# Self-attention, cross-attention and the weight preparation of a decoder merged into one pipeline of 16 items

## The reference

```python
# block 1: a decoder layer on normalised x
def mha(q_in, k_in, v_in, Wq, Wk, Wv, bv, causal):    # 16 heads of 16
    q, k, v = q_in @ Wq, k_in @ Wk, v_in @ Wv + bv     # per head
    scores = q @ k.T * 16 ** -0.5
    if causal: scores = where(tril, scores, -inf)
    return softmax(scores) @ v                         # heads side by side
h = layernorm(x)
h1 = layernorm(mha(h, h, h, *self_weights, causal=True) + h) * g1 + be1
h2 = layernorm(h1 + mha(h1, ctx, ctx, *cross_weights, causal=False)) * g2 + be2
x = x + (layernorm(h2 + relu(h2 @ Wf1 + bf1) @ Wf2 + bf2) * g3 + be3)
# block 2: 8 experts (silu(h W1) * (h W3)) W2, the best 2 of each row
# block 3: attention of each row to the one context row it scores best with (through Wkv), then Wc
# block 4: 16 routed experts of one 256x256 matrix, softmax shares of the best 2, and the mean of two shared ones
```

## Time and profile before

| | us |
|---|---|
| three runs, median (lowest to highest) | 1650.26 (1638.63 to 1658.85) |
| the profiled execution, its own time | 1641.78 |
| its span, first to last instruction | 1640.0 |
| mean granted clock of TensorE in it | 0.857 of full |

### The profile page before, as it was taken

One profiled execution on the slowest core, in us unless ns is written; L12 is line 12 of the kernel. 1 busy time (PEld: TensorE's weight loads), 2 busy tenths in 40 slices (PEclk: granted clock), 3 DMA queues, 4 the chain that ended last, 5 costly groups with the idle time before them and its releaser, 6 DMA issues. The chain is left out here.

```text
span 1640.0 us, 26017 instructions
## 1 busy us (share of the span) xinstructions
PE 1221.0 (74%) x9362; PEld 809.1 (49%) x9362; DVE 1002.6 (61%) x2708; ACT 592.2 (36%) x1145; POOL 348.8 (21%) x521
## 2 busy tenths in 40 slices
PE   3168887389884988305999999993069998599998
PEld 3035553255541776204777777773035554245454
DVE  4747665367772443405888888884446664377776
ACT  4115444045551642004565655651015555000000
POOL 2203335001112235461121211214510100010100
PEclk9989777589995998557999999997558988699999
DMA  9333231333312124327566565633512211101000
GB/s 349 110 90 98 78 90 37 90 104 92 116 60 54 55 85 142 119 92 270 187 216 211 194 236 193 213 116 110 186 48 63 76 44 38 52 27 33 27 13 14
DMA packets 128406, 181.56 MB, mean 111 GB/s; under 512 B 14083, under 2 KB 98838, under 8 KB 124310
## 3 DMA queue, kind: packets, MB, share of 16 engines
q1 hardware_dynamic: 121702, 159.92, 29.7%
q0 software_dynamic: 3584, 8.92, 1.8%
q10 hardware_dynamic: 2992, 11.06, 1.7%
HBM read 131.42 MB, written 48.23 MB: 110 GB/s over the span
## 5 line engine op out<-in xcount | busy, mean ns | idle before, releaser
L1427 PE MATMUL moe_ps_u<-moe_x_hl,moe_up_hl 128*128 128x256 f16 x1932 | 226.5, 276 | 39.7 <-DVE moe_up_hl L1495 31.6
L1427 PEld LDWEIGHTS moe_ps_u<-moe_x_hl,moe_up_hl 128*128 128x128 f16 x1932 | 184.6, 99 | 81.7 <-DVE moe_up_hl L1495 38.0
L1770 PE MATMUL mix_ps_e<-wr_hl,mix_u_hl 128*128 128x512 f16 x768 | 173.5, 382 | 0.0
L1495 DVE SCALAR_TENSOR_TENSOR moe_up_hl<-moe_up_in,moe_up_hl 128x512 f16<-128x512 f32 x161 | 103.9, 679 | 54.5 <-ACT moe_up_hl L1476 54.5
L1539 POOL CAST moe_mid_hl<-moe_mid 128x256 f16<-128x256 f32 x161 | 68.4, 425 | 314.4 <-DVE moe_mid L1510 314.4
L1882 DVE SCALAR_TENSOR_TENSOR mix_acc<-mix_ps_e,mix_shares,mix_acc 128x256 f32<-128x256 f32 x256 | 110.4, 477 | 40.2 <-PE mix_ps_e L1770 39.8
L1476 ACT ACTIVATE moe_up_hl<-moe_up_in 128x512 f16<-128x512 f32 x161 | 99.2, 619 | 62.1 <-DMA moe_up_in<-in_moe_w 62.1
L1770 PEld LDWEIGHTS mix_ps_e<-wr_hl,mix_u_hl 128*128 128x128 f16 x768 | 75.1, 98 | 84.2 <-issue 2.5
L752 DVE TENSOR_REDUCE memory_neg_m<-memory_ps_s 128x2 f32<-128x512 f32 x128 | 84.3, 689 | 48.9 <-PE memory_ps_s L529 46.4
L1439 PE MATMUL moe_ps_y<-moe_down_hl,moe_mid_hl 128*128 128x256 f16 x966 | 109.0, 273 | 0.0
L752 DVE TENSOR_REDUCE cross_neg_m<-cross_ps_s 128x2 f32<-128x512 f32 x128 | 83.5, 687 | 39.1 <-PE cross_ps_s L529 35.9
(11 more groups left out here) (311 smaller groups left out, 2207.2 us busy)
## 6 DMA issues: line engine op xcount, KB each, us to landing
moe_up_in<-in_moe_w SPq DMA_DIRECT2D x23, 1792.0 KB, 7.5
moe_down_in<-in_moe_w SPq DMA_DIRECT2D x23, 896.0 KB, 4.6
xs<-zeros SPq DMA_DIRECT2D x8, 736.0 KB
moe_x_in<-xs SPq DMA_DIRECT2D x23, 256.0 KB, 4.5
ys<-moe_y SPq DMA_DIRECT2D x23, 256.0 KB, 7.9
prep_raw<-in_mix_wr ACTq DMA_DIRECT2D x4, 1024.0 KB, 22.2
self_q_st<-self_q_dram SPq DMA_DIRECT2D x48, 64.0 KB, 2.6
self_k_st<-self_k_dram SPq DMA_DIRECT2D x48, 64.0 KB, 2.6
```

The costliest lines, as they stand in the source:

```text
L1427: mm = nc.tensor.matmul(bank[:, m, :], up_hl[t.slot][:, w, m, dc, f * P:(f + 1) * P], x_hl[t.slot][:, x, dc, :], start=(dc == 0 and w == x ...
L1495: nc.vector.scalar_tensor_tensor(up_hl[t.slot][:, LO, :, :, at].rearrange("p m c h -> p (m c) h"), up_in[t.slot][:, :, :, at].rearrange("p ...
L1770: mm = nc.tensor.matmul(ps_e[fill % RING][:, :, :], u_hl[t.slot][:, r, dc, k * P:(k + 1) * P], wr_hl[:, m, dc, 2 * q:2 * q + 2, :], start= ...
```

## The change

`prepare`, `attention` "self" and `attention` "cross" become one block, `decoder`. Its items are 16: 0 to 7 are the batches of the self-attention, 8 to 15 those of the cross-attention. The pipeline with its two leading and two trailing steps runs once (steps -2 to 17); step 7, for instance, does the shifted scores of the last self item beside the plain scores of the first cross item.
- The rows of all batches stay in SBUF (`rows`, 8 x 256 x 256, float32) from x to `feed_forward`; the loads and stores of h0, x1 and x2 are gone. The split context stays in SBUF too (and is stored once, for the memory attention).
- An eighth on TensorE: both heads of plain scores, then the shifted pair, then one or two of the other parts. At most one part at a time goes to each of two shared banks: ps_near (turned rows, Q, K, V, and the table's rows) and ps_far (values, turned maxima, turned outputs). ps_t is doubled (4 banks), ps_o is gone.
- V is copied by ScalarE, without the bias. GpSimd adds the bias to the residual rows instead, and adds the residual (before: VectorE).
- x is normalised and the weights are split inside the pipeline: the first three matrices before it, the 12 other pieces of 512 columns (cross-attention, memory query, two feed-forward matrices) one per step: ScalarE multiplies by 64 and takes the high part, GpSimd the low part. The context is split batch by batch (ScalarE, GpSimd). The table's 64 matmuls stand in step 1, p = 6.
- `feed_forward` reads the resident rows and loads none.
- The 19 remaining pieces (the memory output matrix, the centroids of 32 columns, the mean of the two shared experts, 16 pieces of the routed experts) move into `experts`, one per tile: SP loads two inputs, GpSimd adds them, ScalarE multiplies by 32 and takes the high part, GpSimd the low part.

Core of the diff (`...` where lines are left out):

```diff
-def prepare(nc, c, x, normed, ctx_t, ctx_hl, wkv, table, matrices, shared, shared_hl):
+def decoder(nc, c, x, ctx_t, wkv, layers, others, rows, ctx_hl, ctx_dram, table):
...
+        ITEMS = LAYERS * BATCHES
+        LEAD, TAIL = 2, 2
+        STEPS = range(-LEAD, ITEMS + TAIL)
...
+        ps_t = ring(ps, "ps_t", [P, 2, BANK])
+        ps_s = ring(ps, "ps_s", [P, TT, SEQ])
+        ps_near = ps("ps_near", [P, 2, SEQ])
+        ps_far = ps("ps_far", [P, BANK])
...
+                pe.wait_ge(ones_set, 4)
+                for t in STEPS:
+                    nxt, new, old = t + 1, t + 2, t - 1
+                    for p in range(PAIRS):
+                        if within(nxt):
+                            scores(nxt, 2 * p)
+                            scores(nxt, 2 * p + 1)
+                        if within(t):
+                            shifted_scores(t, p)
+                        if p == 0 and within(old):
+                            values(old, GROUPS - 1)
+                        if p == 1 and within(t):
+                            turn_maxima(t, 1)
+                        if p in (2, 6) and within(old):
+                            turn_outputs(old, (p - 2) // 4)
+                        if p in (3, 5, 7) and within(t):
+                            values(t, (p - 3) // 2)
+                        if p == 4 and within(nxt):
+                            turn_maxima(nxt, 0)
+                        if p == 0 and within(new):
+                            turn_rows(new)
+                        if p == 1 and within(new):
+                            project(QUERY, new, 0)
+                        if p == 2 and within(new):
+                            project(KEY, new, 1)
+                        if p == 5 and within(nxt):
+                            project_values(nxt)
+                        if p == 6 and t == TABLE_AT:
+                            memory_rows()
...
+                row_stats(0)
+                first_low(0)
+                row_norm(0)
+                first_low(1)
+                row_stats(1)
+                nc.vector.memset(kv_rows[:, :, :], 0.0).then_inc(cleared, 1)
...
+                    for p in range(PAIRS):      # GpSimd
+                        if within(t) and causal(t):
+                            select(t, p)
...
+                        if p == 2 and within(older):
+                            root(older)
+                        if p == 3 and t + LEAD < BATCHES:
+                            context_low(t + LEAD)
+                        if p == 5 and within(older):
+                            gain(older)
+                        if p == 6 and within(older):
+                            shift(older)
+                        if p == 6 and within(t):
+                            add_bias(t)
+                        if p == 7:
+                            for n in range(FIRST, len(pieces)):
+                                if piece_at(n) == t:
+                                    low_part(n)
+                            if within(old):
+                                add_residual(old)
...
-def feed_forward(nc, c, x2, x, w1_hl, b1, w2_hl, b2, gain, shift, gate, out, out_normed, logits, xs, zeroed):
+def feed_forward(nc, c, rows, x, w1_hl, b1, w2_hl, b2, gain, shift, gate, out, out_normed, logits, xs, zeroed):
...
-                    pe.wait_ge(x2_loaded[t.slot], 16 * (t.turn + 1))
...
-def experts(nc, c, xs, w13, w2, tile_expert, ys):
+def experts(nc, c, xs, w13, w2, tile_expert, ys, matrices):
...
+                    n = t.n - 1                  # ScalarE, at the end of a tile
+                    if 0 <= n < len(pieces):
+                        srcs, hl, at, w = pieces[n]
+                        r = raw[0][n % STAGES][:, 0:w]
+                        act.wait_ge(raw_summed, n + 1)
+                        nc.scalar.activation(r, r, ACT.Copy, scale=LIFT / 2).then_inc(lifted, 1)
+                        act.wait_ge(lifted, n + 1)
+                        nc.scalar.copy(hl[:, HI, at:at + w], r).then_inc(piece_hi, 1)
...
                         nc.gpsimd.tensor_copy(mid_hl[t.slot][:, HI, f, :], mid[:, f, :]).then_inc(mid_hi, 1)
+                        if f == 1 and 0 <= t.n - 2 < len(pieces):
+                            n = t.n - 2
+                            w = pieces[n][3]
+                            pool.wait_ge(raw_loaded[n % STAGES], 32 * (n // STAGES + 1))
+                            nc.gpsimd.tensor_tensor(raw[0][n % STAGES][:, 0:w], raw[0][n % STAGES][:, 0:w], raw[1][n % STAGES][:, 0:w],
+                                                    ALU.add).then_inc(raw_summed, 1)
+                        if f == 4 and 0 <= t.n - 3 < len(pieces):
+                            n = t.n - 3
+                            _, hl, at, w = pieces[n]
+                            pool.wait_ge(piece_hi, n + 1)
+                            nc.gpsimd.tensor_tensor(hl[:, LO, at:at + w], raw[0][n % STAGES][:, 0:w], hl[:, HI, at:at + w],
+                                                    ALU.subtract).then_inc(piece_split, 1)
```

More of the change, by code:

```diff
@@ L63, in pipeline, with __init__ @@
         step(Turn(0, n, count))
+class Layer:
+    def __init__(self, weights, bias, gain, shift):
+        self.weights, self.bias, self.gain, self.shift = weights, bias, gain, shift
 class Constants:
@@ new lines, in decoder, with piece_at, flat @@
+        highs = {}
+        for kind, n in near:
+            if kind in (TURN, QUERY, KEY):
+                highs[kind, n] = len(highs) + 1
+        FIRST = 3
+        pieces = [(src, 0, hl) for src, hl in layers[0].weights]
+        pieces += [(src, at, hl) for src, hl in layers[1].weights + others for at in range(0, src.shape[1], 2 * D)]
+        STAGES = 4
+        def piece_at(n):
+            return n - FIRST - LEAD
+        def flat(hl):
+            return hl[:, :, :, :].rearrange("p l c f -> p l (c f)")
@@ new lines, in _ @@
+                load_x(0)
+                load_piece(0)
+                load_piece(1)
+                load_x(1)
+                load_piece(2)
+                load_x(2)
+                for layer in range(LAYERS):
+                    for dst, vec in ((bv, layers[layer].bias), (g, layers[layer].gain), (be, layers[layer].shift)):
+                        sp.dma_start(dst[layer][:, :], vec.partition_broadcast(P)).then_inc(params_loaded, 16)
+                for b in range(3, BATCHES):
+                    load_x(b)
@@ new lines, in project_values @@
+                def project_values(n):
+                    weights_ready(n, 2)
+                    pe.wait_ge(near_emptied, near[VALUE, n])
+                    wt, frm = layers[n // BATCHES].weights[2][1], source(n, 2)
+                    for k in range(TT):
+                        for dc in range(DC):
+                            for r, m in PRODUCTS:
+                                mm = nc.tensor.matmul(ps_near[:, k, :], frm[:, r, dc, k * P:(k + 1) * P], wt[:, m, dc, :],
+                                                      start=(dc == 0 and m == r), stop=(dc == DC - 1 and r == LO))
+                    mm.then_inc(near_filled, 1)
@@ new lines, in values @@
+                def values(n, gr):
+                    if causal(n):
+                        pe.wait_ge(selected, PAIRS * n + 2 * gr + 2)
+                    else:
+                        pe.wait_ge(exps_done, PAIRS * n + 2 * gr + 2)
+                    if gr == 0:
+                        pe.wait_ge(near_emptied, near[VALUE, n] + 1)
+                    pe.wait_ge(far_emptied, far[PV, gr, n])
+                    for k in range(TT):
+                        a, b = queries_of(n, k)
+                        at = at_of(n, k)
+                        for j in range(GROUP):
+                            h = GROUP * gr + j
+                            mm = nc.tensor.matmul(ps_far[j * VW:(j + 1) * VW, a:b], v[n % 2][:, k, h, :],
+                                                  probs[h // 2 % 4][:, h % 2, at:at + b - a], start=(k == 0), stop=(k == TT - 1),
+                                                  tile_position=(0, j * VW))
+                    mm.then_inc(far_filled, 1)
@@ L202, in _, with high_part @@
[L202 to L208 removed]
+                def high_part(n):
+                    _, at, hl = pieces[n]
@@ L257, in _ @@
[L257 to L263 removed]
+                for k in range(2):
+                    nc.vector.memset(v[k][:, :, :, HD:VW], 0.0).then_inc(ones_set, 1)
+                dve.wait_ge(ones_set, 2)
```

636 lines of the change are left out of this document (485 added, 151 removed).

## The result

The change takes 1585.91 us (median of 4 runs, 1583.03 to 1597.08) against 1645.36 (median of 4, 1638.63 to 1658.85): ratio 0.964, 95% interval 0.956 to 0.972. The forecast was 1568, with a range of 1512 to 1612. The profiled execution took 1583.03 us, 58.8 less than that of before.

A forecast was written before the change was run, and what follows sets the result against it. TensorE was taken to bound the full attention steps, with waits and a reduced clock, and TensorE with VectorE the experts. From 1641.8 us, 121 less before the feed-forward, 46 more in the experts and 1 for scatter gave 1568, range 1512 to 1612.

The forecast's parts named there:

- item starts that stay 22 or more apart: Decoder steps: sign that the forecast time is wrong; the item starts were expected 21 us apart.
- both heads' scores wait only for maxima of the eighth before: TensorE's new order in a step: with ps_t doubled, old waits go; steps of 21.0 us causal, 20.4 cross.
- the steps don't shorten: Rival, decoder steps: single near and far banks and GpSimd in p = 6 bring new waits; 17 us more, 1585; chance 0.13.
- fewer pauses: Clock in decoder steps: small bonus, taking causal steps as 21.0 us and cross steps, computed at 20.8, as 20.4.
- The rule of the Trainium skill: TensorE's clock: throttled by default, released by activity; a pipeline with fewer pauses would hold 2.4 GHz.
- The end: Decoder's last two steps and end 44 us instead of 49.4, then 6.5 us to the feed-forward's first matmul.
- The experts: GpSimd's two instructions per weight piece hold VectorE: 2.0 us per tile, 36 us; with lower clock 46 us.
- further 10 us for a falling clock: Experts: TensorE's idling lowers its granted clock; up to 30 us possible, 10 us taken.
- the experts pay nothing: Rival, experts: GpSimd's operations find gaps or wait themselves; time 1522; chance 0.17.
- the experts fall to half clock: Rival, experts: half clock for part of each tile, 20 us more or above; time 1590; chance 0.1.
- Full clock: Rival, merged decoder steps: TensorE holds full clock once pauses shrink; 26 us less, 1542; chance 0.13.
- Slower: Rival, decoder: TensorE stays at 1.2 GHz through the steps, making the kernel slower than before; chance 0.02.

The follow-up runs named there:

- both edits: Changed kernel with VectorE's low parts of the turned rows taken after both maxima and GpSimd's bias added at p = 1: 1552.02 us, ratio 0.933.
- The run with the waits put back: Changed kernel with SP's two old waits (rows turned, bias added) again before its feed-forward loads of a tile: 1614.0 us, ratio 0.975.
- one changed kernel: Changed kernel with TensorE's eighth in the order of before and the bias early: 1552.96 us, ratio 0.941; memory attention 216.4 us.

## Why the prediction was right, and where it was not

The time came out 18 us above the forecast and inside its range, and the terms of the sum say that this is partly luck: the steps missed by 38 us, and the experts and the feed-forward, which missed the other way, brought 40 back. By the prediction's own sign, item starts that stay 22 or more apart, its account of the steps is wrong.

- **Start and fill.** First rows 17.27 for 16; step 0 at 61.46 for 57. Of the 4.5 missing, 1.3 are in the start and 2.8 in the filling steps, 44.2 us for the 40.4 + 1 that I had let stand.
- **The steps: the part that failed.** The step at fault is "both heads' scores wait only for maxima of the eighth before". At p = 0 one of those maxima is queued on VectorE behind the rows' cut, and I had followed the turned rows only to Q (0.4 us), not to the maximum behind them. Steps of 24.1 and 23.1 for 21.0 and 20.4 make 8 x 3.1 + 5 x 2.7 = 38 us. With that pause and the `select`'s gone, they are 19.9 and 20.2, and t = 0 to 13 takes 282.0, where the sum had 8 x 21.0 + 10 + 5 x 20.4 = 280. In kind this is the rival "the steps don't shorten" (1585), but they grew, by 2.0 and 1.3 us, and that rival named one bank each and GpSimd in p = 6. GpSimd's wait is there, six times in six causal steps, 8.0 us together, up to the 1.5 I had priced. Taking it away alone gave 5 to 8 us. The larger wait, which both kinds of step have, nobody had named.
- **The clock.** I took it as a mean carried over (0.84 and 0.94) and "fewer pauses" as a small bonus. In the new order the runs show it as about half of the matter: one pause a step left or both, 0.74 to 0.83 in the causal steps; neither, 0.88 to 0.93 in three runs. The rule of the Trainium skill that I had set beside the sum (TensorE: Matmul & The Clock Gate, Part 1: activity releases the throttle) comes near the runs with both edits; in the change, 149 to 151 us is full activity at half clock.
- **The table.** 9.5 us longer (33.6 in step 1 against 24.1) for 10.
- **The end.** From t = 13 to the feed-forward 70.6 for 20.4 + 44 + 6.5 = 70.9.
- **The experts.** The mechanism was right and is now shown by leaving the work out and by moving it. The size was 31 for 36 (1.7 us per tile for 2.0: the two instructions that VectorE has meanwhile are held by 1.07 and 0.64). The further 10 us for a falling clock were wrong: 0.97 before and after.
- **The feed-forward.** I counted only the load that ends. The term left out is SP's queue: a wait in front of it held back all that was behind. The run with the waits put back shows 19 to 21 of the 24 us. I had written of SP only that no queue grows, and put the stage at 0.
- **Memory attention.** The 12 us are not explained. The code is the same and TensorE's busy time is longer at the lower clock (179 at 0.78, 194 at 0.71). The same stage took 216 to 231 us in kernels that share the change, in the batch with the fast kernel before, and 238 to 255 in the two batches with the slower one. So it varies by more than 12 without any edit to it, and one changed kernel had less than before. Whether the change has a part in it stays open.

Rivals: "the experts pay nothing" fell (30.2 us), and so did "the experts fall to half clock" (0.97 before and after). "Full clock" did not come in the causal steps of the change (0.82), nor quite with both edits; the cross steps reached 0.97 in two of five traces of the unedited decoder. "Slower" fell with the ratio of 0.964.

## What to carry to other kernels

When work is moved up in one engine's order, list for each thing it waits for what stands in front of that on the producer's queue: here the scores were moved in front of Q, and behind one VectorE instruction that waited for a third engine. Two pauses of TensorE in one step must be judged together: either one removed gave about its own length, both gave 10 to 16 us more than these two gains in 11 steps, through the clock. And work for GpSimd costs VectorE nothing if it begins at VectorE's last instruction before a pause and ends near its first one after it; bind it there by a semaphore, not to a place in its own loop.

## What was not expected of the hardware

- In the feed-forward's steady tiles a load issued by SP directly behind the 736 KB of zeros took 4.5 to 5.6 us to issue, 3.1 and 3.6 us when the zeros had left some 4 us before, and 0.4 us when they had left 9 us or more before.
- Identical decoders took 317 to 326 us from t = 0 to t = 13 in five traces, with clocks of 0.74 to 0.83 in the causal steps; the experts, at 0.97, agreed within 0.9 us in eight (412.8 to 413.7).
